# Routed attention without a query projection: query and key weights multiplied per head on the chip

## What is computed

```python
q_top, q_idx = jax.lax.top_k(einsum('bnd,gd->bgn', x, w_qr), 128)
kv_top, kv_idx = jax.lax.top_k(einsum('bnd,gd->bgn', x, w_kvr), 64)
q = einsum('bgnd,ged->bgne', x[bidx, q_idx], w_q)              # 8 heads of 64
k, v = split(einsum('bgnd,ged->bgne', x[bidx, kv_idx], w_kv))  # 8 heads of 64
v = v * sigmoid(kv_top)
k, v = concat([null_k, k]), concat([null_v, v])                # one null key a head
attn = softmax(einsum('bghid,bghjd->bghij', q, k) * 64 ** -0.5)
o = einsum('bgne,gde->bgnd', attn @ v, w_out) * sigmoid(q_top)
out = mean over the groups that chose the token, or null_token where none did
```

## Time and profile before

| | us |
|---|---|
| median of 3 runs | 2942.31 |
| the runs | 2936.19 to 2942.46 |
| profiled execution | 2945.98 |
| its span, first to last instruction | 2944.2 |
| busy: PE, DVE, ACT, POOL | 2626.4, 1947.8, 1401.5, 1086.1 |
| mean granted clock of TensorE | 0.949 |

### The profile page before, as it was taken

One profiled execution on the slowest core, in us unless ns is written; L12 is line 12 of the kernel. 1 busy time (PEld: TensorE's weight loads), 2 busy tenths in 40 slices (PEclk: granted clock), 3 DMA queues, 4 the chain that ended last, 5 costly groups with the idle time before them and its releaser, 6 DMA issues. The chain is left out here.

```text
span 2944.2 us, 62888 instructions
## 1 busy us (share of the span) xinstructions
PE 2626.4 (89%) x24286; PEld 1750.9 (59%) x24286; DVE 1947.8 (66%) x4549; ACT 1401.5 (48%) x2887; POOL 1086.1 (37%) x1384
## 2 busy tenths in 40 slices
PE   7999789989699879897887899997999989889998
PEld 2344457756467656465555577774666657556665
DVE  7888746757566677634774577765777747557775
ACT  5555234456244335322663355544555545445653
POOL 4787545324345313313112434430222346312223
PEclk9899789999799989889999999998999999999999
DMA  2000200011000001100111000002222211112221
GB/s 85 1 1 0 82 22 23 10 26 31 26 19 23 5 3 50 70 29 19 31 24 32 17 1 1 1 1 69 62 91 71 69 32 31 61 46 77 78 88 49
DMA packets 62020, 107.28 MB, mean 36 GB/s; under 512 B 7978, under 2 KB 46582, under 8 KB 60960
## 3 DMA queue, kind: packets, MB, share of 16 engines
q1 hardware_dynamic: 56352, 94.80, 10.6%
q0 software_dynamic: 5376, 8.47, 1.0%
HBM read 80.17 MB, written 23.86 MB: 35 GB/s over the span
## 5 line engine op out<-in xcount | busy, mean ns | idle before, releaser
L617 ACT ACTIVATE s_sT<-s_R 128x1024 f32<-128x1024 f32 (+2 forms) x448 | 402.6, 945 | 180.4 <-PE s_R L548 180.2
L659 DVE TENSOR_REDUCE s_negm<-s_R 128x4 f32<-128x1024 f32 (+1 forms) x320 | 359.5, 1166 | 88.9 <-PE s_R L517 87.0
L517 PE MATMUL s_R<-s_qk 32*128 32x256 f32 (+2 forms) x3584 | 243.1, 384 | 46.2 <-ACT s_sT L617 25.3
L548 PE MATMUL s_R<-s_qA,s_qk 32*128 32x256 f32 (+2 forms) x3584 | 240.9, 382 | 12.4 <-DVE s_negm L659 7.2
L568 PE MATMUL s_OB<-s_sT,s_v 128*32 128x256 f32 (+2 forms) x3584 | 224.5, 368 | 7.5 <-ACT s_sT L617 3.8
L691 DVE TENSOR_TENSOR s_qA<-s_qk,s_OB 128x256 f32<-128x256 f32 x224 | 94.4, 421 | 201.3 <-PE s_OB L591 193.7
L517 PEld LDWEIGHTS s_R<-s_qk 32*128 32x128 f32 x3584 | 155.3, 186 | 103.5 <-issue 67.1
L548 PEld LDWEIGHTS s_R<-s_qA,s_qk 32*128 32x128 f32 x3584 | 164.5, 185 | 65.1 <-issue 55.8
L624 ACT ACTIVATE s_oc<-s_OB 128x256 f32<-128x256 f32 x224 | 85.8, 383 | 230.1 <-PE s_OB L568 229.8
L1599 POOL TENSOR_TENSOR s_pr<-s_pr,s_rinv 128x1024 f32<-128x1024 f32 x64 | 121.1, 1892 | 186.5 <-DVE s_rinv L1710 186.5
L2940 POOL TENSOR_TENSOR all_hT<-s0s_hs,s0s_cb 128x1024 f32<-128x1024 f32 x64 | 150.7, 2354 | 29.7 <-PE s0s_Y L2887 14.3
(11 more groups left out here) (614 smaller groups left out, 6267.6 us busy)
## 6 DMA issues: line engine op xcount, KB each, us to landing
s_wB<-enc_b SPq DMA_DIRECT2D x32, 962.5 KB, 4.7
s_scratch<-s_pk SPq DMA_DIRECT2D x58, 256.0 KB, 2.0
s_qk<-s_scratch SPq DMA_DIRECT2D x232, 64.0 KB
s_wA<-enc_a SPq DMA_DIRECT2D x32, 194.0 KB, 4.1
big<-moe SPq DMA_DIRECT2D x2, 2347.0 KB, 10.7
big<-routed SPq DMA_DIRECT2D x2, 2312.0 KB
all_W<-weights SPq DMA_DIRECT2D x1, 2201.0 KB, 16.4
all_W<-weights SPq DMA_DIRECT2D x1, 2200.5 KB, 11.7
```

Source lines behind the costliest of these rows:

```text
L517: last = pe.matmul(S[h][:, a.keys_at(t)], b.qk[rows, r % 2, 0, c, t * P:(t + 1) * P], b.qk[rows, r % 2, 1, c, lo:hi], start=(t == 0), stop ...
L548: last = pe.matmul(b.R[:, a.turned_at(u, h // 2), :][:, h % 2, a.at(kt)], b.qk[rows, r % 2, 1, c, kt * P:(kt + 1) * P], b.qA[rows, u % 2, ...
L617: act.activation(b.sT[:, u % (a.lag + 1), 2 * p:2 * p + 2, 0:a.width], b.R[:, a.turned_at(u, p), 0:a.width], ACT.Exp).then_inc(s.expd, 1)
L659: return dve.tensor_reduce(b.negm[:, u % 2, :, at].rearrange("p t h -> p h t"), S[:, :, 0:a.key_width].rearrange("p h (t k) -> p h t k", t ...
```

## The change

Scores are (x_q Wq)(x_k Wk)^T = x_q (Wq Wk^T) x_k^T. The first stage now multiplies, for each of 4 expert groups and 8 heads, the key and query weights to a 128x128 matrix in PSUM, copied to `wqk`; and the query weights with each null key, copied to `tnull`. For that both weights are packed with the 64 features of a head as rows, two heads above each other. In the second stage the key items compute, for each head, `wqk` times the gathered key rows (four items a group, two in the third and two in the fourth step), `kT` holds eight heads of 128 rows, and a unit's scores are two products whose stationary operand is `sel`, the gathered query rows. The "q" items, their copies and `qT` are gone.

```diff
--- before.py
+++ after.py
@@ -3008,17 +3008,14 @@
         for i in range(self.UNITS + self.TAIL):
             items = []
             if i == 0:
-                items += [("keys", 0)] + self.front(0, "k") + [("queries", 0)] + self.front(0, "q")
+                items += [("keys", 0)] + [("k", 0, k) for k in range(4)] + [("queries", 0)]
             if i < self.UNITS:
                 nxt = i // self.NB + 1
                 if nxt < self.GROUPS and i % self.NB:
-                    items += self.front(nxt, ("gather", "q", "k")[i % self.NB - 1])
+                    what, lo = (("gather", 0), ("k", 0), ("k", 2))[i % self.NB - 1]
+                    items += [(what, nxt, k) for k in (lo, lo + 1)]
             self.steps.append(items)
         self.number = {item: n for n, item in enumerate(item for s in self.steps for item in s)}
-
-    @staticmethod
-    def front(group, what):
-        return [(what, group, k) for k in range({"gather": 2, "q": 4, "k": 2}[what])]
 
     def gathered(self, u):
 
@@ -3041,6 +3038,7 @@
     U, NB, G, H, DH, NQ, NK = plan.UNITS, plan.NB, plan.G, 8, 64, 128, 64
     ROWS = B * 2 * G
     wq, wk, wv, wo = g.big("r_wq"), g.big("r_wk"), g.big("r_wv"), g.big("r_wo")
+    nk = g.big("r_nk")
     with Stage(nc, name) as st:
         sig = st.sb("sig", [P, 2, ROWS])
         place = st.sb("place", [P, ROWS])
@@ -3049,6 +3047,8 @@
         rcount = st.sb("rcount", [P, TT, B])
         missed = st.sb("missed", [P, TT, B])
         nw = st.sb("nw", [P, 4, D])
+        wqk = st.sb("wqk", [P, 4, 2, 4, D])
+        tnull = st.sb("tnull", [P, 2, 4, 4])
         first_kv = st.sb("first_kv", [NK, ROWS], mybir.dt.uint32)
         hq = st.sb("hq", [P, 2 * NB, D])
         hk = st.sb("hk", [P, 2 * NB, D])
@@ -3093,8 +3093,8 @@
             ST = sr.ps("ST", [P, 512])
             HT = sr.ps("HT", [P, 4, 512])
             NW = sr.ps("NW", [P, 512])
-            loaded, turned, hT_cp, nw_mm = [
-                sr.sem(n) for n in ("loaded", "h_turned", "hT_cp", "nw_mm")]
+            loaded, turned, hT_cp, nw_mm, wqk_mm, wqk_cp = [
+                sr.sem(n) for n in ("loaded", "h_turned", "hT_cp", "nw_mm", "wqk_mm", "wqk_cp")]
             logits, lg_ready, rows_ready, sorted_, mask_ready, back, counted, steps, stored = [
                 sr.sem(n) for n in ("logits", "lg_ready", "rows_ready", "sorted", "mask_ready", "back", "counted",
                                     "steps", "stored")]
@@ -3161,10 +3161,32 @@
                                              g.big("r_nvc")[:, 4 * s + c:4 * s + c + 1].to_broadcast([P, P]),
                                              wo[:, (4 * s + c) * P:(4 * s + c + 1) * P], start=(c == 0), stop=(c == 3))
                     last.then_inc(nw_mm, 1)
+                    for s in range(4):
+                        if s >= 2:
+                            pe.wait_ge(wqk_cp, s - 1)
+                        for c in range(4):
+                            for par in range(2):
+                                rows = slice(par * DH, (par + 1) * DH)
+                                at = slice((4 * s + c) * D, (4 * s + c + 1) * D)
+                                last = pe.matmul(HT[:, 2 * (s % 2) + par, c * D:(c + 1) * D], wk[rows, at], wq[rows, at],
+                                                 start=True, stop=True, skip_group_check=True,
+                                                 tile_position=(par * DH, 0))
+                        last.then_inc(wqk_mm, 1)
+                    pe.wait_ge(wqk_cp, 3)
+                    for s in range(4):
+                        for c in range(4):
+                            for par in range(2):
+                                rows = slice(par * DH, (par + 1) * DH)
+                                at = slice((4 * s + c) * D, (4 * s + c + 1) * D)
+                                last = pe.matmul(HT[:, par, (4 * s + c) * 4:(4 * s + c + 1) * 4], wq[rows, at],
+                                                 nk[rows, 4 * s:4 * s + 4], start=True, stop=True,
+                                                 skip_group_check=True, tile_position=(par * DH, 0))
+                    last.then_inc(wqk_mm, 1)
                     pe.wait_ge(half_found, 1)
                     pe.transpose(ST[0:NK, 2 * ROWS:3 * ROWS], found_f[:, 0:NK], g.ident[0:ROWS, 0:ROWS])\
                       .then_inc(half_back, 1)
                     pe.wait_ge(steps, 36)
+                    pe.wait_ge(wqk_cp, 5)
                     keep_busy(pe, g, HT[:, 0, :], 16)
                     pe.wait_ge(sorted_, 1)
                     pe.transpose(ST[:, 0:ROWS], found_f[:], g.ident[0:ROWS, 0:ROWS]).then_inc(back, 1)
@@ -3187,6 +3209,13 @@
                         act.activation(g.hT[:, r * T:(r + 1) * T], HT[:, r % 4, 0:T], ACT.Copy).then_inc(hT_cp, 1)
                     act.wait_ge(nw_mm, 1)
                     act.activation(nw[:].rearrange("p s d -> p (s d)"), NW[:], ACT.Copy)
+                    for s in range(4):
+                        act.wait_ge(wqk_mm, s + 1)
+                        act.activation(wqk[:, s, :, :, :].rearrange("p q c d -> p q (c d)"),
+                                       HT[:, 2 * (s % 2):2 * (s % 2) + 2, :], ACT.Copy).then_inc(wqk_cp, 1)
+                    act.wait_ge(wqk_mm, 5)
+                    act.activation(tnull[:], HT[:, 0:2, 0:64].rearrange("p q (s n) -> p q s n", s=4)[:, :, :, 0::5],
+                                   ACT.Copy).then_inc(wqk_cp, 1)
                     act.wait_ge(back, 2)
                     act.activation(sig[:].rearrange("p k r -> p (k r)"), L[:, 0:2 * ROWS], ACT.Sigmoid)
 
@@ -3232,8 +3261,7 @@
         with Stage(nc, name + "a") as sa:
             sel = sa.sb("sel", [P, 2, NB, NQ + NK])
             warm = sa.sb("warm", [P, 1])
-            qT = sa.sb("qT", [P, 2, 4, NB, NQ])
-            kT = sa.sb("kT", [P, 2, 4, NB, NK + 1])
+            kT = sa.sb("kT", [P, 2, H, NB, NK + 1])
             v = sa.sb("v", [P, 3, 4 * DH])
             ev = sa.sb("ev", [P, 2, 2, 4, NK + 1])
             mx = sa.sb("mx", [P, 2, 2, 4])
@@ -3288,20 +3316,12 @@
                                 pe.transpose(f[:, at:at + NQ], hq[:, ring, :], g.ident[:])
                                 pe.wait_ge(got_k[ring], 16 * (u // (2 * NB) + 1))
                                 last = pe.transpose(f[:, at + NQ:at + NQ + n], hk[0:n, ring, :], g.ident[0:n, 0:n])
-                        elif it[0] == "q":
-                            _, group, c = it
-                            s = plan.unit(group * NB)[0]
-                            pe.wait_ge(f_cp, copied("gather", group, 1) if group else copied("queries", 0))
-                            last = pe.matmul(f, wq[:, (4 * s + c) * P:(4 * s + c + 1) * P], sel[:, group % 2, :, 0:NQ],
-                                             start=True, stop=True)
                         else:
                             _, group, k = it
                             s = plan.unit(group * NB)[0]
-                            if group == 0:
-                                pe.wait_ge(f_cp, copied("keys", 0))
-                            for c in (2 * k, 2 * k + 1):
-                                last = pe.matmul(f[:, (c % 2) * 256:(c % 2 + 1) * 256],
-                                                 wk[:, (4 * s + c) * P:(4 * s + c + 1) * P],
+                            pe.wait_ge(f_cp, copied("gather", group, 1) if group else copied("keys", 0))
+                            for hd in (2 * k, 2 * k + 1):
+                                last = pe.matmul(f[:, (hd % 2) * 256:(hd % 2 + 1) * 256], wqk[:, s, hd // 4, hd % 4, :],
                                                  sel[:, group % 2, :, NQ:NQ + NK], start=True, stop=True)
                         last.then_inc(f_mm, 1)
 
@@ -3314,15 +3334,14 @@
                             items = []
                         if i < U:
                             group = i // NB
-                            pe.wait_ge(f_cp, copied("k", group, 1) if group else copied("q", 0, 3))
+                            pe.wait_ge(f_cp, copied("k", group, 3) if group else copied("queries", 0))
                             pe.wait_ge(nullk, group + 1)
                             if i >= 1:
                                 pe.wait_ge(v_cp, i)
-                            for h in range(H):
-                                rows = slice((h % 2) * DH, (h % 2 + 1) * DH)
-                                pe.matmul(S[:, h % 2, (h // 2) * (NK + 1):(h // 2 + 1) * (NK + 1)],
-                                                 qT[rows, group % 2, h // 2, i % NB, :],
-                                                 kT[rows, group % 2, h // 2, i % NB, :], start=True, stop=True)
+                            for par in range(2):
+                                pe.matmul(S[:, par, 0:4 * (NK + 1)], sel[:, group % 2, i % NB, 0:NQ],
+                                          kT[:, group % 2, 4 * par:4 * par + 4, i % NB, :], start=True, stop=True,
```

(13 more changed lines are left out.)

## The result

| | before | after |
|---|---|---|
| median of the runs, us | 2942.31 | 2900.5 |
| the runs, us | 2936.19 to 2942.46 | 2893.3 to 2903.58 |
| profiled execution, us | 2945.98 | 2898.08 |
| its span, us | 2944.2 | 2896.4 |
| mean granted clock | 0.949 | 0.953 |

The ratio is 0.9862, with a 95% interval of 0.9846 to 0.9879: 41.8 us faster between the medians. The forecast was 2912 in a range of 2899 to 2925, 30 us faster; the time lies in the range, but only 1.5 us above its low end, and at the number of rival B (2901); the forecast's own sum was 11 us short of the gain.

What follows compares the result with a forecast made beforehand. PE's own work was taken as the bound. Per instance, steady groups -13.7, group 0 -2.0, attention start -2.6 and sort +3.0 make -15.3 us, -30.6 in all: 2911.7, say 2912 us, range 2899 to 2925.

Steps and rivals of the forecast that it cites:

- rival B: Clock stays up under the null keys (+1.3) and group 0 escapes part of its low stretch (-4): 2901 us, chance 0.14.
- The bound: Steady attention groups: PE's own work sets the period, with steps of 4.2, 5.1, 6.0 and 6.0 us after the change.
- Items: Steady group: four query products go and key items double from two to four, together -1.81 us a group.
- Scores: Each unit's scores as four full-array passes of 0.229 us, 0.92 instead of 1.04 us: a gain of 0.12 a unit.
- DVE as the next bound: Step with no item: DVE needs 4.34 us against PE's 4.22; gain kept in groups 1 to 6, 0 in the last.
- The sort's stage: New products on PE delay the turning of the half ranks: +3.0 us an instance, bounds +1.3 and +9.4.
- Group 0: First group's units, with part at the low clock: -2.0 us an instance, bounds -1.0 and -3.5.
- The start of the attention: Further key items come ahead of the queries, query products go, first scores come earlier: -2.6 us, bounds 1.8 and 3.5.
- A: Sort held longer, new products at the low clock throughout: +9.4 in place of +3.0 us, 2924.5 us, chance 0.12.
- C: Steady steps: PE no longer ends last in the item steps, half of the steady gain, 2926 us, chance 0.05.
- D: Scores in 64 units: full-array pass costs the lost packing, 2.08 us a unit instead of 1.04; 2985 us, chance 0.03.
- E: About nothing changes: ranks turned 15 to 18 us late, packed products not overlapping; 2936 to 2943 us, chance 0.03.

## Why the prediction was right, and where its terms were wrong

**The bound, right.** PE without a gap before, without a gap after, and the steps as foretold: 4.2, 5.1, 6.0, 6.0 against 4.19, 5.06, 5.96, 5.96.

**Items, right to the hundredth.** -1.81 us a group; packed scores in the changed kernel isolate it at 23.61 - 21.80 = 1.81.

**Scores, right in sign, low by a quarter.** 0.12 us a unit was forecast from the key items' 0.229 us a pass. The passes measured 0.22, but the 0.10 us for going over to the values' products comes on top, so the stretch is 0.98 us and not 0.92, and by itself gains only 0.06. The other 0.09 to 0.10 is the going over to packed products, which stands in the rows of the output projection ahead of them and not in those of the scores. I read the cost of the packed scores from their own start to the next start, and what they did to the instruction ahead of them fell out. Start to start of the whole step would have held it. With 0.15 to 0.16 a unit in steps of steady groups, the steady group is 2.44 us shorter, not 2.29; the first two of the six take 21.39 and 21.31 us instead of 21.17. There DVE adds the null token, and its rounds come at 5.42 us after the change too, as in the kernel without query items; that this is what the 0.2 and 0.1 us are for was not tested.

**DVE as the next bound, misread.** I took the 4.34 us between two maxima with no idle ahead of the second for DVE's own round. The rows of after refute it; the empty step, DVE:

```profile
474.58 0.70 DVE L3499 TENSOR_REDUCE s1a_mx<-s1a_S 128x8 f32<-128x520 f32 x1 [0.35 <-PE s1a_S L3349]
...
476.71 0.70 DVE L3508 TENSOR_REDUCE s1a_rsum<-s1a_ev 128x8 f32<-128x520 f32 x1 [0.31 <-ACT s1a_ev L3430]
...
478.84 0.69 DVE L3499 TENSOR_REDUCE s1a_mx<-s1a_S 128x8 f32<-128x520 f32 x1
```

The maxima follow at 4.26 us, again with no idle time ahead of the second. The round can be no longer than that, and DVE waits 0.31 us for ACT within it; before, it was 4.34 because PE came every 4.34. In the last group, where all steps are empty, three of them take 12.80 us after the change, 4.27 on average, against 4.19 for an empty step of a steady group. That would fit a DVE round of 4.26 that binds there, but no row of PE shows a wait for it, so it isn't shown. The group gains 0.26 us where I had 0; it cost the sum next to nothing.

**The sort's stage, a term that failed: +3.0 forecast, +0.1 to +0.3 measured in after** (a hold of 0.24 and 0.28 us counted from the sort's start; up to 1.4 in other executions). Two errors of one sign. The queue: I had the null keys' last pass 360.3 - 346.09 = 14.2 us behind the sort's start at the full clock; it came 357.09 - 344.04 = 13.05 behind it, as ACT's two copies took 0.97 each instead of 1.02, the products ahead of them ended 0.4 earlier, and the 64 passes took 3.9 us instead of 4.2 (3.6 with the clock up throughout, 56 ns a pass, where I had taken the 65 of the packed scores; those 65 hold a change of packing). The clock: I placed its fall 2.4 us into the null keys, after the row of the 8-column router products; it fell after 3.25 us in after's first instance, after 3.2 and 4.6 in the kernel with twice the products, and not at all in after's second. With the lower bound, +1.3, the sum would have been 1.7 us an instance nearer. The row that I took as nearest was of wider products of another form, with PE idle for a third of the us in which the clock fell; these leave PE no gap.

**Group 0, mis-sized: -2.0 forecast, -5.7 and -4.3 measured, the largest miss together with the sort's.** The work's share is 1.82, near the forecast; the rest is the clock, 3.86 of it in the first instance. The prediction had the 4 us as a bound and as rival B, and argued against it that the gap of 2.02 us stays. The gap did stay (394.25), and the long fall did not come, so the gap is not enough for it. Packed scores bring the long fall back, filler in the gap takes it away, with the gap and full scores it costs 0 to 2.2 us: these three are shown. By what the chip decides it is open.

**The start of the attention, right within its bounds:** -2.6 against -3.3 and -2.7.

**The tail, missed:** +0.8 and +1.4 where I had nothing. 0.6 to 1.5 us is a fall of the clock behind a gap of 2.04 us. The gap was in before too, the fall was not; but in the kernel with the new products alone, whose attention is that of before, both tails have the fall (25.48 and 25.34 us against 23.93 and 23.80). So whether it belongs to the change is open. With it gone, last group and tail take 12.80 + 24.39 = 37.19 and 12.79 + 24.28 = 37.07 us against 36.99 before (13.06 + 23.93). So what PE gains in the last group is given back behind it, as it would be if DVE, at 4.26 a step, ended last there; that was not tested by itself.

**Rivals.** B is what happened, nearly in both parts: null keys under the full clock but for their last 0.7 us in one instance, group 0 without most of its low stretch. It had 0.14; its evidence was as good as that of the forecast. That the time is in the range at all is thanks to the range reaching to B: each of the two clock terms was off by about 3 us an instance, to the same side. The mean of the terms as measured, -0.2 + 3.0 + 5.0 + 14.3 - 1.1 = 21 us an instance, gives 42. A (sort held +9.4), C (half of the steady gain), D (full scores at twice the packed ones' time) and E (no change) fall; D by the packed scores, A and E by the products alone in the kernel before.

## What to carry to other kernels

Cost a group of instructions from the start of the work ahead of it to the start of the work behind it: a change of the array's tiling shows in the neighbour's rows. When a product can be made with fewer, wider passes, the packing of short ones into row halves is no argument against it; and where a stage begins with gaps, ask first whether the clock falls in it, since eight products of filler in each instance gave 6 us without touching the work. Filler that once covered a wait should be taken out once the wait is gone: in this kernel that was worth 6.7 us by the rows, 9.4 by the medians.

## What the runs showed of the hardware

- Row-packed passes of 64 rows and 65 columns, fp32: the two of a pair start 0.01 us apart, pairs follow at 0.11 us. Full-array passes of 260 columns: 0.22 us. Going over from full-array to row-packed products, or from either to column-packed ones: 0.1 us each time.
- Passes of 64 rows and 4 columns, packed in halves: 3.60 us for 64 at the full clock, 56 ns each, in pairs every 0.11 us; those of 128 columns, packed alike, also follow in pairs at 0.11 us. The granted clock stayed at 1.00 for 3.2 to 4.6 us of them, or until their end after 3.6, and at 0.50 a pass took 0.10 us (40 in 4 us).
- With the gap left open, group 0 takes 24.0 to 24.3 us with packed scores in six of six and 18.5 to 20.7 with full ones in six of six; with filler in the gap 18.53 or 18.54 in four of four. The same kernel had the short fall in one execution and not in another.
- A gap of 2.04 or 2.05 us in the tail was followed by a low clock in after and in the kernel with the new products alone, and not in before.
- No idle time ahead of a DVE row doesn't prove that DVE is at its floor: one round of the same instructions took 4.34 us before and 4.26 after, with no gap ahead of the second maximum in either.
